# The stage between two attentions: a new order of work on all engines, and one sum split between VectorE and GpSimd

## The reference

```python
s = _L0_attn_ref(xn, L0_attn_W_qkv, L0_attn_W_out)   # ends with: out @ W_out
g = _silu(_L0_ffn_ref(xn, ...))                      # ends with: rows + sum of two gated expert rows
x = x + s * g                                        # the code's x_all = fg * s_all + xs
xn = _layernorm(x)
q, k, v = xn @ Wq, xn @ Wk, xn @ Wv                  # for the second attention
y = xn @ quantised(kernel) + bias + xn @ a @ b       # gated later with silu
```

## Time and profile before

| what | value |
|---|---|
| median of 3 runs (lowest to highest) | 2787.17 us (2784.41 to 2787.22) |
| the profiled execution, its own time | 2794.57 us |
| its span | 2792.8 us |
| granted TensorE clock over the span | 0.963 |
| busy: TensorE, VectorE, ScalarE, GpSimd | 2610.0, 2260.1, 1598.7, 998.8 us |

### The profile page before, as it was taken

One profiled execution on the slowest core, in us unless ns is written; L12 is line 12 of the kernel. 1 busy time (PEld: TensorE's weight loads), 2 busy tenths in 40 slices (PEclk: granted clock), 3 DMA queues, 4 the chain that ended last, 5 costly groups with the idle time before them and its releaser, 6 DMA issues. The chain is left out here.

```text
span 2792.8 us, 48909 instructions
## 1 busy us (share of the span) xinstructions
PE 2610.0 (93%) x19041; PEld 1239.3 (44%) x19041; DVE 2260.1 (81%) x4726; ACT 1598.7 (57%) x2599; POOL 998.8 (36%) x542
## 2 busy tenths in 40 slices
PE   7998999999999996799998788899999999999999
PEld 4665333333333335566666444333333333333337
DVE  7987999999999968678884677698888888878753
ACT  3543467777777785434442445356666666666660
POOL 1000001101110110421200430167888888789890
PEclk9998799999999997899999899899999999999999
DMA  4242212321232113442310368322020220202203
GB/s 140 72 102 81 50 25 46 70 55 34 54 70 55 54 34 115 99 101 72 117 56 30 124 191 224 95 61 63 16 69 13 69 73 9 69 13 73 76 9 128
DMA packets 143719, 203.06 MB, mean 73 GB/s; under 512 B 14480, under 2 KB 110176, under 8 KB 140528
## 3 DMA queue, kind: packets, MB, share of 16 engines
q1 hardware_dynamic: 133072, 175.34, 23.0%
q0 software_dynamic: 9056, 24.59, 4.2%
q10 hardware_dynamic: 1360, 0.01, 0.0%
HBM read 123.34 MB, written 76.02 MB: 71 GB/s over the span
## 5 line engine op out<-in xcount | busy, mean ns | idle before, releaser
L779 POOL TENSOR_TENSOR at_probs<-at_probs 128x2048 f32<-128x2048 f32 (+3 forms) x205 | 726.5, 3549 | 153.7 <-PE at_acc L959 137.3
L816 ACT ACTIVATE at_probs<-at_st 128x512 f32<-128x512 f32 (+3 forms) x1280 | 588.1, 539 | 335.6 <-PE at_st L903 181.2
L330 DVE TENSOR_REDUCE at_part<-at_s 128x1 f32<-128x512 f32 (+3 forms) x1280 | 688.4, 602 | 46.1 <-PE at_s L369 20.5
L311 ACT ACTIVATE at_probs<-at_st 128x1024 f32<-128x1024 f32 (+3 forms) x640 | 542.2, 898 | 236.4 <-PE at_st L396 138.1
L837 DVE TENSOR_REDUCE at_part<-at_s 128x1 f32<-128x512 f32 x768 | 501.4, 683 | 83.8 <-PE at_s L895 80.6
L831 DVE CUSTOM_DVE_ANT_0 at_s<-at_s,at_later 128x384 f32<-128x384 f32 (+3 forms) x512 | 247.9, 498 | 73.9 <-PE at_s L895 67.0
L448 PE MATMUL at_acc<-at_probs,at_v 128*32 128x512 f32 (+3 forms) x2560 | 302.9, 550 | 0.1
L895 PE MATMUL at_s<-all_k,all_q 96*128 96x512 f16 (+3 forms) x640 | 209.2, 362 | 9.4 <-PEq L43 4.8
L903 PE MATMUL at_st<-all_q,all_k 98*128 98x512 f16 (+3 forms) x640 | 204.0, 352 | 4.4 <-DMA all_q<-at_strip 4.1
L903 PE MATMUL at_st<-at_qT,at_kT 98*128 98x512 f16 (+3 forms) x640 | 201.5, 350 | 4.4 <-DMA at_qT<-at_strip 4.3
L369 PE MATMUL at_s<-lin_k_first,lin_q_first 48*128 48x512 f16 (+3 forms) x640 | 189.9, 377 | 14.9 <-DVE at_part L330 7.6
(11 more groups left out here) (378 smaller groups left out, 3935.4 us busy)
## 6 DMA issues: line engine op xcount, KB each, us to landing
att<-at_otile SPq DMA_DIRECT2D x64, 256.0 KB, 2.1
lin_w_raw<-in_W SPq DMA_DIRECT2D x16, 1024.0 KB
at_v<-v SPq DMA_DIRECT2D x11, 1024.0 KB, 10.7
v<-pr_vt SPq DMA_DIRECT2D x32, 256.0 KB
exp_out<-ex_ot SPq DMA_DIRECT2D x32, 256.0 KB
v<-p_vt SPq DMA_DIRECT2D x32, 256.0 KB, 4.1
p_xs<-in_x SPq DMA_DIRECT2D x8, 512.0 KB, 5.2
qhi<-p_parts SPq DMA_DIRECT2D x8, 512.0 KB
```

The lines of the kernel that those rows point to most:

```text
L311: act.activation(probs[:, quad % RING, heads_down * p:heads_down * (p + 1), off:QB], st_ps[n % st_slots][:, :, off:QB], ACT.Exp, scale=EXP ...
L330: dve.tensor_reduce(part[:, w % 2, qt * HG + h, j:j + 1], s_ps[n % S_SLOTS][:, 0:width], AX.X, ALU.max).then_inc(item_free, 1)
L779: pool.tensor_tensor(total, total, probs[:, slots.slot[quad], :, off:QB], ALU.add).then_inc(add_done, 1)
L816: act.activation(probs[:, slots.slot[quad], h, off:QB], st_ps[n % ST_SLOTS][:, off:QB], ACT.Exp, scale=EXP_SCALE).then_inc(exp_done, 1)
```

## The change

- TensorE's list: three turns ahead (`AHEAD`), four buffers for turned pairs in place of two (`TURNS`), 11 pairs before block 0 (9 of them with the next turn behind, `FIRST`); the other five `s 11` to `s 15` stand in blocks 0 to 4 between `qB` and `kA`, with the next turn behind each. `T b+1` stands between `vA` and `vB` and no longer behind `vB`.
- VectorE and GpSimd: `x b` becomes a product on VectorE (`times b`) and an addition on GpSimd (`add`), which stands in front of the gathers of block b+2. `moments b` waits for `added`.
- VectorE's and ScalarE's lists are written anew: one mixed tile between `lo qA` and `lo qB`, three behind `lo kB`; `statistics b+1` at the head of block b; the output of block b at its end; the SiLU of `y` one block later.
- SyncE: the four weights are loaded first, then the input blocks; `load_group` also waits for `s 15`, since the turned pairs lie in its target. GpSimd's first gathers wait for nothing, and the maximum over partitions stands before tile 6.

```diff
-    PAIRS = NT // 2
+    PAIRS, FIRST, AHEAD, TURNS = NT // 2, 9, 3, 4
+    late = {b: m for b, m in enumerate(range(FIRST + 2, PAIRS))}
...
-        nT = carried.v[:, 0:8, :].rearrange("p (m t c) n -> p m t c n", m=2, t=2)
+        nT = carried.v[:, 0:4 * TURNS, :].rearrange("p (m t c) n -> p m t c n", m=TURNS, t=2)
...
+            for n, (name, behind) in enumerate((("Wq", "nT 1"), ("Wk", "s 0"), ("Wv", "s 1"))):
+                pe_s.wait(sp, behind)
...
+                    pe_s.wait(sp, f"s {PAIRS - 1}")
                     carried.load_group(sp, C, qk_out, v_out)
...
+            def add(b):
+                dve_s.wait(pool, f"times {b}")
+                pool.wait_ge(x_ld[b % 2], 16 * (b // 2 + 1))
+                pool.tensor_tensor(x_all[:, 4 * b:4 * b + 4, :], fg[:, b % 2, :, :], xs[b % 2][:, :, :],
+                                   ALU.add).then_inc(added, 1)
+
             for n in range(NT):
                 b, t = n // 4, n % 4
+                if t == 0 and b >= 2:
+                    add(b - 2)
+                if n == 6:
+                    pool.wait_ge(maxed, 4)
+                    pool.partition_all_reduce(top[:, :], most[:, :], P, bass.bass_isa.ReduceOp.max).then_inc(shared, 1)
...
+            for m in range(AHEAD):
+                linear(m)
+            for m in range(FIRST):
                 output(m)
-                if m == 9:
+                linear(m + AHEAD)
+                if m == 3:
                     silu(0)
-                if m == 12:
+                if m == 4:
+                    upper_weights(0)
+                if m == 6:
                     deviation(0)
...
-                link(tt(fg[:, b % 2, :, :], fg[:, b % 2, :, :], s_all[:, cols, :], ALU.mult))
-                dve.wait_ge(x_ld[b % 2], 16 * (b // 2 + 1))
-                step(f"x {b}", tt(x_all[:, cols, :], fg[:, b % 2, :, :], xs[b % 2][:, :, :], ALU.add))
+                step(f"times {b}", tt(fg[:, b % 2, :, :], fg[:, b % 2, :, :], s_all[:, cols, :], ALU.mult))
...
+            for b in range(NB):
+                if b + 1 < NB:
+                    statistics(b + 1)
+                lower(0, "q", "A", b)
+                if b + 2 < NB:
+                    mixed_tile(b + 2, 0)
+                lower(0, "q", "B", b)
...
+                    if side == 0 and b in late:
+                        project(late[b])
+                        if late[b] + 1 < PAIRS:
+                            linear(late[b] + 1)
```

More of the change, by code:

```diff
@@ new lines, in combine_and_project @@
+    pe_names = [f"nT {m}" for m in range(AHEAD)]
+    for m in range(FIRST):
+        pe_names += [f"s {m}", f"nT {m + AHEAD}"]
+    pe_names += ["T 0", f"s {FIRST}", f"s {FIRST + 1}"]
+    for b in range(NB):
+        pe_names += [f"qA {b}", f"qB {b}"]
+        if b in late:
+            pe_names += [f"s {late[b]}"] + [f"nT {late[b] + 1}"] * (late[b] + 1 < PAIRS)
+        pe_names += [f"kA {b}", f"kB {b}", f"vA {b}"] + [f"T {b + 1}"] * (b + 1 < NB) + [f"vB {b}", f"y {b}"]
+    act_names = [f"nT {m}" for m in range(AHEAD)]
@@ L2578, in combine_and_project @@
             c.sem(n) for n in ("bias_ld", "maxed", "shared", "scaled", "upper_w", "lower_w"))
+        added = c.sem("added")
         part_out, v_kept, ch = (c.sem(n) for n in ("part_out", "v_kept", "ch"))
         pe_s, act_s, dve_s = Marks(c.sem("pe"), pe_names), Marks(c.sem("act"), act_names), Marks(c.sem("dve"), dve_names)
[L2581 to L2584, removed]
+        turning = ("nT", "T")
+        rot = Banked(c, "rot", [(n, reader(n)) for n in pe_names if n.split()[0] in turning], 1)
+        banks = Banked(c, "bank", [(n, reader(n)) for n in pe_names if n.split()[0] not in turning], 3)
         block = c.block()
@@ L2639, in _ @@
                     ).then_inc(got[n % 8], 16)
-                if n == 7:
-                    pool.wait_ge(maxed, 4)
-                    pool.partition_all_reduce(top[:, :], most[:, :], P, bass.bass_isa.ReduceOp.max).then_inc(shared, 1)
+            for b in range(NB - 2, NB):
+                add(b)
         @block.scalar
@@ L2740, in mixed_tile @@
                     step(f"mixed {b}", last)
-            def mixed(b):
-                for t in range(4):
-                    mixed_tile(b, t)
             def combine(b):
@@ L2881, in turn, with product @@
                 step(f"T {b}", mm)
-            for m in range(PAIRS + 2):
-                if 0 < m <= PAIRS:
-                    linear(m - 1)
-                if m == PAIRS + 1:
-                    turn(0)
-                if m > 1:
-                    project(m - 2)
+            for m in range(AHEAD):
+                linear(m)
+            for m in range(FIRST):
+                project(m)
+                linear(m + AHEAD)
+            turn(0)
+            project(FIRST)
+            project(FIRST + 1)
+            def product(b, job, of):
+                d = banks.take(pe, f"{job} {b}")
+                for y in range(2):
+                    for n in range(NF):
+                        for of_w, of_x in TERMS:
+                            left, right = of(2 * "AB".index(job[1]) + y, of_w, of_x, n)
+                            mm = pe.matmul(d[:, y, :], left, right, start=n == of_w == of_x == 0,
+                                           stop=n == NF - 1 and of_x == 1)
+                step(f"{job} {b}", mm)
             for b in range(NB):
```

258 lines of the change are left out of this document (109 added, 149 removed).

## The result

Before 2786.8 us (median of 4 runs, the three shown above and one more, 2784.41 to 2787.22), after 2763.11 us (4 runs, 2758.18 to 2766.86): ratio 0.9916, 95% interval 0.9898 to 0.9933. That is faster by 0.8%, clear of the noise, and inside the range; the forecast of 2754 is 9 us too low. The profiled execution after took 2761.82 us, its span 2760.0.

The account below looks back on a forecast made before the run. Steady blocks were taken as bound by VectorE's order, the list phase by lateness. Terms -21.5 - 21 + 6 = -36.5 us, hand-overs give back 3: -33, so profiled 2794.57 to 2761.6, median 2754; range 2736 to 2774.

Parts of the forecast that it names:

- the hand-overs: Between engines, two in each of six blocks at about 0.25 us, left out of the sum: give back 3 us.
- List phase: Before block 0: earlier gathers and weights and fewer pairs let q start at 35.8 in place of 57.4 us, -21.5 us.
- the open price: GpSimd's configuration change in front of the first addition, on the list phase's path: 0.3 to 14 us, taken as 0.3.
- The first addition starts late: Rival, chance 0.12: the configuration change takes 7 us in the list phase, everything behind z 0 slips, 2761 us.
- The row at 2.34 us: Earlier profile row where an operation follows a GpSimd configuration change after 0.29 us of idle time, used for the 0.3.
- Blocks 0 to 4: They go at TensorE's pace, four at 21.3 us and the fifth at 20.8: 107.5 in place of 128.5, -21 us.
- The 1.5 us for block 0: Added to block 0 for lower weights and an exposed addition in VectorE's list.
- The rival that VectorE sets the pace: Chance 0.13: `moments` waits for the whole addition in blocks 0 to 4, each loses 2.4 us, +12, 2766 us.
- Block 5: ScalarE waits for block 4's k stores, which land 15.6 us into block 5: 30.6 in place of 24.5, +6 us.
- the queue drains in time: Rival, chance 0.2: gathers and stores interleave better, block 5 isn't held, 2742 us.
- here the queue of stores comes in: In block 5: SyncE's group request delays block 4's k stores, landing about 26 us after the request before the change.
- The end and blocks 6 and 7: No change: TensorE has no gap to lose in those blocks, and the last stores still follow `vB 7`.

Follow-up runs that it names:

- the kernel with the tiny addition: The changed kernel plus one unread 128x4 addition on GpSimd, right behind the maximum over partitions and ahead of the gathers of tiles 6 and 7: 2761.06 us, one run.
- experiment 3: Four edits of the changed kernel: group load on GpSimd's queue 2758.88 us, separate q and k store semaphores 2756.56, load cut in four 2746.31, whole load later 2754.76.
- own semaphores: The changed kernel with one semaphore for the q stores and one for the k stores: 2756.56 us, ratio 0.9908 to before.
- pairs in the list: The changed kernel with four of the five moved pairs back in the list phase, one staying in block 0: 2763.33 us, ratio 0.9931 to before.
- group cut in four: The changed kernel with its group load in four parts, behind the v stores of blocks 4, 5, 6 and 7: 2746.31 us, ratio 0.9869 to before.
- GpSimd's queue: The changed kernel with the second attention's first group loaded by GpSimd's queue behind the last gathers, in place of SyncE's: 2758.88 us, ratio 0.9918 to before.
- whole group later: The changed kernel with the whole group load behind block 4's v stores, in place of ahead of its q stores: 2754.76 us, ratio 0.9896 to before.
- the split kernel: The changed kernel with the additions of blocks 0 and 1 on VectorE and those of blocks 2 to 7 on GpSimd: 2749.7 us, ratio 0.988 to before.

## Why the prediction was right, and where it was off

Three of the four terms held within 3 us; the sum of the stage was off by 6 us (its terms add up to -33.5, written as -33), and the median by 9. That it wasn't more is luck: the blocks gained 2 us more than forecast and the hand-overs didn't cost their 3, and these two took back half of the 10 us that the list phase missed. It is luck too that the profiled execution came to 2761.82, next to the forecast's 2761.6: of its 32.8 us, 5.2 lie ahead of the stage. The step from there to the median, 7.4 us off, fits before and not after, where the profiled execution is 1.3 us below the median.

- *List phase, -21.5 forecast, -11.5 measured.* The step that failed is the open price: "So it costs 0.3 to 14 us, on the path of the list phase. I take 0.3". It measured 7.0 us, as the rival "The first addition starts late" had it, and the time of that rival, 2761, is nearer than the forecast's 2754. The row at 2.34 us was the wrong neighbour: another operation, with no maximum over the partitions ahead of it. (What follows the other change, at 1063.09, is a product and not an addition; it waited for a transfer, so its row couldn't show the price.) The Trainium skill (GPSIMD Engine Reference, Instruction dispatch) says that a first call to a freshly loaded kernel pays about 6 us; 7.0 here and 8.06 in the kernel with the tiny addition are of that size and somewhat longer. The trace shows only the change of configuration at the start of this time, 37 ns long, and no row in the rest of it; what is loaded there no row shows. Against the forecast's steps, counted from the stage's start: the 12 gathers end at 15.3 (forecast 15.2); the shared result is used at 19.1 (17.5), because Wv's maximum ended at 17.0 and not at 15; the gathers end at 22.7 (21); the addition at 32.0 (23.4); z 0 at 38.5 (29.9); q starts at 45.9 (35.8). So 1.7 us are from the weights, 6.9 from the addition, 1.8 from T 0 and the two pairs, less 0.3: the forecast's own steps add up to 35.5, and the 0.3 to its 35.8 is as much as the price that it took. The 1.8 was a misreading: the row at 1528.14 is one pair (x8) at the low clock and not two; two took 5.72.
- *Blocks 0 to 4, -21 forecast, -23.0 measured.* TensorE's pace, as counted: 21.2 for 21.3, the last 20.76 for 20.8. The 1.5 us for block 0 and the 3 for hand-overs were not needed: VectorE waited 4.7 us for GpSimd's additions over five blocks, and TensorE is busy throughout (block 1 in the windows; the other four are the same). The rival that VectorE sets the pace fell with it.
- *Block 5, +6 forecast, +7.75 measured.* `hi qA 5` went 16.7 us into the block (forecast 15.6), and TensorE stood 11.24 us at kB, ended by `lo qA`, as said. The group went at 7.2 us into block 4 (8.9 forecast) and needed 30.3 us to klo's landing (1658.18 to 1688.46, when ScalarE goes on), not 27.5, so that the two errors nearly cancel. That the queue drains in time fell; that it is SyncE's queue, as "here the queue of stores comes in" has it, fell too (experiment 3): it is the load on the DMA engines.
- *The end and blocks 6 and 7* stayed, as said.

The medians differ by 23.7 us and the stage by 26.8. In the other runs the median shows between 0.6 us more and 6 us less than the stage; the profiled execution of before was 7.4 above its median, and the rest of the kernel varies between 1013.5 and 1018.7 us from trace to trace without a change in it. This rest isn't explained.

What stays open: why the transfers of the group move at about 215 GB/s and those behind them at 380, and why the change of configuration takes 7.0 in one kernel and 8.06 in another. Part of it is spread: in the five other kernels that have the first addition where after has it, GpSimd stood 6.86 us (own semaphores), 7.16 (pairs in the list), 7.24 (group cut in four), 7.34 (GpSimd's queue) and 7.77 (whole group later). And the tiny addition stands directly behind the maximum, whose result after is used 2.0 us after its start though its row has 0.39, so part of the 8.06 may be the maximum's own.

That additions keep the configuration once it is made is shown (one change for six to eight additions). That a maximum undoes it, at a like price, shows in after ahead of this stage, where GpSimd goes from products (at 1068.79) back to the maximum of line 2209:

```profile
L2209 POOLq MODIFY_POOL_CONFIG  x4: 1/20/37, 1019.8 to 1164.9; - x4
```

```profile
1170.99 0.37 POOL L2209 PARTITION_ALL_REDUCE lin_top<-lin_most  x1 [6.42 <-issue]
```

The last change stands at 1164.9, and the maximum begins 6.1 us later, 1.5 us after its operand is ready at 1169.51. In the trace before the same maximum waited 13.93 us for VectorE, which covered it.

## What to carry to other kernels

An operation can have a price of its own when it follows one of another kind, as an addition behind a maximum over the partitions has here: look for where it will stand first, not only for what it costs each time, and put it where the engine waits anyway. A stall that other stalls covered appears in full when these are removed: ask of each large transfer what will be queued on the DMA engines when the work around it gets faster, and cut it into pieces that fit between the stores that are waited for. An average price hides both; one trace by stages shows them.

## What the runs showed of the hardware

In this stage GpSimd changed its configuration once, at the first addition behind a maximum over the partitions, and stood 6.86 to 8.06 us in the traces of seven kernels, unless it was waiting for something else (12.47 us, where the same change cost nothing). The way back, from products to a maximum, stood 6.42 us. Gathers between maximum and addition ran without a change (the first one after began at 1537.95, right behind the maximum). In the split kernel the change was made when the addition came up in GpSimd's list, 12.3 us before its operand was ready. And with a group of 4 MB asked for from GpSimd's queue ScalarE waited 16.2 us for a store of SyncE's queue, as long as with the group in SyncE's queue.
